# The last head prepares the next stage, values copied at mid-head, and a new order of turns, norms and transposes

## The reference

```
q, k, v = xn @ W_qkv                          # split in 16 heads
attn    = softmax(q k^T / 4 + spatial_bias)   # bias on tokens 1..256 alone
s       = (attn v) @ W_proj + b + layernorm(xn)
```

```
q, k, v = shift(x) @ wqkv
q, k    = rotary(l2norm(q) * qs), rotary(l2norm(k) * ks)
x       = x + softmax(mask(8 q k^T)) v @ wo
x       = x + (a * gelu(g)) @ w2 + b2,   a, g = layernorm(shift(x)) @ w1 + b1
```

## Time and profile before

| | us |
|---|---|
| median of 3 runs (lowest, highest) | 3201.47 (3199.73, 3202.40) |
| the profiled execution's own time | 3198.47 |
| its span, first to last instruction | 3196.5 |
| PE busy | 3056.0 (96%) |
| DVE busy | 2384.1 (75%) |
| ACT busy | 2236.8 (70%) |
| POOL busy | 846.4 (26%) |

### The profile page before, as it was taken

The page is one execution under the profiler, slowest core; times in us unless marked ns, Lnnn a source line. Parts: engine busy times, 40 slices in busy tenths (PEclk is TensorE's granted clock), DMA queues, the critical chain, the costliest instruction groups (busy, mean ns, idle before and its releaser), DMA issues.

```text
span 3196.5 us, 94351 instructions
## 1 busy us (share of the span) xinstructions
PE 3056.0 (96%) x37280; PEld 1985.2 (62%) x37280; DVE 2384.1 (75%) x4554; ACT 2236.8 (70%) x4645; POOL 846.4 (26%) x945
## 2 busy tenths in 40 slices
PE   8899999999999999999789999999999999999998
PEld 5444454444444444444367777777777777777776
DVE  8799989999899999899656666656665666656664
ACT  4588888888888888888556655665566556655564
POOL 5300000000000000000144434444344444444443
PEclk9899999999999999999889999999999999999999
DMA  7531111111111111111201100011100111011110
GB/s 236 174 105 49 36 44 45 45 43 40 45 45 45 40 40 48 45 45 35 83 11 42 39 26 29 28 41 39 31 26 30 38 39 34 25 33 33 41 38 4
DMA packets 157768, 153.48 MB, mean 48 GB/s; under 512 B 18144, under 2 KB 131128, under 8 KB 157496
## 3 DMA queue, kind: packets, MB, share of 16 engines
q1 hardware_dynamic: 157496, 149.52, 14.8%
HBM read 90.73 MB, written 58.72 MB: 47 GB/s over the span
## 4 chain that ended last, share of the span: by engine, by line
PE 85%; ACT 5%; issue 3%; DVE 3%; POOL 2%; SPq 1%; DMA 0%; POOLq 0%; DVEq 0%; ACTq 0%
PE banks L1347 15%; PE banks L1386 14%; PE banks L1403 14%; PE banks L1571 8%; PE banks L1453 7%; PE banks L1583 6%; PE banks L1499 4%; PE banks L1532 4%; PE banks L1542 4%; PE banks L1464 3%; PE banks L1511 3%; ACT kT L879 1%; ACT qT L872 1%; ACT vw L866 1%; PE banks L1521 1%
## 5 line engine op out<-in xcount | busy, mean ns | idle before, releaser
L1056 DVE TENSOR_REDUCE pair_max<-banks 128x1 f32<-128x1024 f32 x1039 | 1259.8, 1222 | 132.6 <-PE banks L1347 79.0
L837 ACT ACTIVATE probs<-banks 128x512 f32<-128x512 f32 x2057 | 1104.2, 599 | 171.5 <-PE banks L1386 164.8
L1347 PE MATMUL banks<-k_aug,q_aug 96*32 96x512 bf16 x8312 | 854.8, 385 | 6.1 <-ACT v_all L807 3.3
L1386 PE MATMUL banks<-q_aug,k_aug 98*32 98x512 bf16 x8228 | 846.8, 382 | 0.0
L1403 PE MATMUL banks<-probs,v_cur 128*32 128x256 f32 x8192 | 630.1, 380 | 31.1 <-POOL probs L614 31.1
L1347 PEld LDWEIGHTS banks<-k_aug,q_aug 96*32 96x32 bf16 x8312 | 239.7, 96 | 370.8 <-DVE pair_max L1056 215.5
L1386 PEld LDWEIGHTS banks<-q_aug,k_aug 98*32 98x32 bf16 x8228 | 251.8, 96 | 191.4 <-issue 3.5
L1571 PE MATMUL banks<-hnT,w_sb 128*114 128x128 f32 x3072 | 363.7, 275 | 0.9 <-ACT hnT L910 0.9
L1403 PEld LDWEIGHTS banks<-probs,v_cur 128*32 128x32 f32 x8192 | 260.7, 111 | 160.1 <-issue 37.9
L1571 PEld LDWEIGHTS banks<-hnT,w_sb 128*114 128x114 f32 x3072 | 344.9, 179 | 22.0 <-ACT hnT L910 22.0
L660 POOL TENSOR_TENSOR norms<-norms,half_power 128x8 f32<-128x8 f32 x128 | 210.3, 1643 | 442.0 <-DVE norms L1154 442.0
(11 more groups left out here) (141 smaller groups left out, 4022.9 us busy)
## 6 DMA issues: line engine op xcount, KB each, us to landing
acc_scratch<-acc_sb SPq DMA_DIRECT2D x128, 256.0 KB, 2.4
heads_win<-acc_scratch SPq DMA_DIRECT2D x512, 64.0 KB
q_aug<-q_parts SPq DMA_DIRECT2D x204, 64.0 KB, 2.2
k_aug<-k_parts SPq DMA_DIRECT2D x204, 64.0 KB, 2.2
q_parts<-parts SPq DMA_DIRECT2D x16, 384.0 KB, 3.0
k_parts<-parts SPq DMA_DIRECT2D x16, 384.0 KB, 3.9
x_in<-in_x SPq DMA_DIRECT2D x10, 512.0 KB, 4.5
xT_scratch<-xnT SPq DMA_DIRECT2D x8, 512.0 KB, 4.8
```

The source lines that it names most:

```text
L837: nc.scalar.activation(probs[:, step % PRING, :], banks[:, (use - first_use) % SRING, :], ACT.Exp, scale=SCALE).then_inc(prob_ready, 1)
L1056: nc.vector.tensor_reduce(pair_max[:, q, half:half + 1], banks[:, 4 + 2 * (t % 2):6 + 2 * (t % 2), :], AX.XY, ALU.max).then_inc(smax_read, 1)
L1347: last = nc.tensor.matmul(banks[m:m + CT, 4 + t % 4, :], q_aug[0:TERM_ROWS, b, q * P + m:q * P + m + CT], k_aug[0:TERM_ROWS, b, kq * BANK: ...
L1386: last = nc.tensor.matmul(banks[m:m + CT, (use - use_of(first_step)) % SRING, :], k_aug[0:AUG, b, kb * P + m:kb * P + m + CT], q_aug[0:AUG ...
```

## The change

It has four parts.

1. **Values.** POOL copies batch 0's values of the next head in the middle of a head, when batch 0's last value product is done; the bias products of batch 0 stand at the head of the loop and wait only for the exponentials.
2. **Last head.** The last turn ends at step 6 behind its head (its last copy of sums), with no scores, maximum tiles or shift rows of a further head.
3. **Seam.** The first windows and the rotary tables are loaded in the last head, behind its fourth group. POOL sets the constants of stage 3 and the tables in the last head. Behind `phase2_end` it zeroes only the first half of `kT` and `vw`, each with a semaphore of its own; `wo_sb` has one too. PE no longer waits for `phase2_end`.
4. **Stage 3.** PE transposes k, then q, then h(k), and projects v behind them. k's transposes go to bank 1, and `scores(0)` takes banks 0 and 1. ACT copies k, q, v in that order and squares q behind `cross`. DVE turns q before it sums its squares, and adds the attention between them. POOL, and no longer DVE, multiplies k by its inverse norms (`scale_k`), and inverts q's eight norms in two halves around the variance.

```diff
-    first = LH // 2 if n == 0 else 0
+    first = 0 if n == 0 else LH // 2
...
-    yield 0, range(FIRST_STEP)
-    for h in range(HEADS):
-        yield h, range(FIRST_STEP, FIRST_STEP + STEPS)
+    yield 0, range(FIRST_STEP), False
+    for h in range(HEADS - 1):
+        yield h, range(FIRST_STEP, FIRST_STEP + STEPS), False
+    yield HEADS - 1, range(FIRST_STEP, STEPS + SUMS_STEP + 1), True
...
+    for group in range(GROUPS):
+        store_sums(HEADS - 1, group)
+        if group == QC - 1:
+            for b in range(B):
+                load_window(0, b)
+            sp.dma_start(tables[:], rotary[0]).then_inc(tables_in, 16)
...
-    sp.dma_start(wo_sb[:], wo.rearrange("l (k p) e -> p l k e", p=P)).then_inc(ff_weights, 16)
+    sp.dma_start(wo_sb[:], wo.rearrange("l (k p) e -> p l k e", p=P)).then_inc(wo_in, 16)
...
     for b in range(B):
-        load_window(0, b)
         load_heads(0, b)
-    sp.dma_start(tables[:], rotary[0]).then_inc(tables_in, 16)
...
+    copy_values(0, 0)
+    pool.wait_ge(bias_ready, 1)
     with nc.gpsimd.Fori(0, HEADS) as h:
+        next_head = nc.gpsimd.snap((h + 1) % HEADS)
+        apply_bias(h, 0)
         pool.wait_ge(pv_done, h * PVH + 1)
-        for b in range(B):
...
+        copy_values(h, 1)
+        apply_bias(h, 1)
+        pool.wait_ge(pv_done, h * PVH + (PVH // 2 + 1))
+        copy_values(next_head, 0)
...
-    nc.gpsimd.sem_inc(phase2_end, 1)
-    pool.wait_ge(phase2_end, 4)
-    nc.gpsimd.memset(kT[:], 0.0).then_inc(ff_const, 1)
-    nc.gpsimd.memset(vw[:], 0.0).then_inc(ff_const, 1)
...
-    pool.wait_ge(ff_const, 10)
+    pool.wait_ge(ff_const, 8)
...
+    pool.wait_ge(ff_weights, FF_WEIGHTS)
+    pool.wait_ge(tables_in, 16)
+    for l in range(LAYERS):
+        rotary_table(l)
     for carried in (k_carried, v_carried, x_carried, x1_carried):
         nc.gpsimd.sem_inc(carried, ITEMS)
     nc.gpsimd.sem_inc(mask_set, 1)
-    pool.wait_ge(ff_weights, FF_WEIGHTS)
+    nc.gpsimd.sem_inc(phase2_end, 1)
+    pool.wait_ge(phase2_end, 4)
+    nc.gpsimd.memset(kT[:, :, :, :, 0:WINDOW], 0.0).then_inc(k_zeroed, 1)
+    nc.gpsimd.memset(vw[:, :, :, 0], 0.0).then_inc(v_zeroed, 1)
...
+    def invert_k(i, k):
+        invert_norms(i, k, 2, LH, 2 * LH)
+    def invert_q(i, k, n):
+        invert_norms(i, k, 4, n * (LH // 2), (n + 1) * (LH // 2))
+    def scale_k(i, k):
+        b = k % B
+        pool.wait_ge(inv_norms, at(i, k, 1, 3))
+        pool.wait_ge(k_added, at(i, k))
+        t8 = turned[:, b, 1].rearrange("p (h d) -> p h d", d=LD)
+        nc.gpsimd.tensor_tensor(t8, t8, norms[:, b, LH:].unsqueeze(2).to_broadcast([P, LH, LD]),
+                                ALU.mult).then_inc(k_turned, 1)
...
-    for l in range(LAYERS):
-        rotary_table(l)
-    invert_norms(0, 0, 1)
-    invert_norms(0, 0, 0)
+    invert_k(0, 0)
+    scale_k(0, 0)
+    for n in range(2):
+        invert_q(0, 0, n)
...
     for i, k, more in items(nc.gpsimd):
         widen_sums(i, k)
         if more:
-            invert_norms(i, k + 1, 1)
-            invert_norms(i, k + 1, 0)
+            invert_k(i, k + 1)
+            scale_k(i, k + 1)
+            invert_q(i, k + 1, 0)
         invert_deviation(i, k)
+        if more:
+            invert_q(i, k + 1, 1)
...
-            act.wait_ge(st_ready, h * ST_USES + (use + 2))
+            if ends and step >= STEPS:
+                if step == STEPS + SUMS_STEP:
+                    save_sums(h, group - 1)
+                continue
+            act.wait_ge(st_ready, h * ST_USES + (use + 2 - (ends and step > STEPS - KB + MSTEP)))
...
+            if kb == MSTEP and not (ends and group + 1 == GROUPS):
...
+        if n == 0:
+            act.wait_ge(q_crossed, at(i, k))
...
+                       banks[:, lanes(b) + 1, :].rearrange("p (j t) -> p j t", t=WINDOW)).then_inc(kT_kept, 1)
...
+            keep_k(i, k + 1)
+            keep_q(i, k + 1)
             keep_v(i, k + 1)
-            keep_q(i, k + 1)
-            keep_k(i, k + 1)
...
+            if ends and tile >= STEPS:
+                continue
...
+        if n == 1:
+            dve.wait_ge(squares_done, at(i, k, 1, 2))
+        else:
+            dve.wait_ge(qk_ready, at(i, k, 2, 2))
...
-        dve.wait_ge(k_added, at(i, k))
-        dve.wait_ge(inv_norms, at(i, k, 1, 2))
-        t8 = turned[:, b, 1].rearrange("p (h d) -> p h d", d=LD)
-        nc.vector.tensor_tensor(t8, t8, norms[:, b, LH:].unsqueeze(2).to_broadcast([P, LH, LD]),
-                                ALU.mult).then_inc(k_turned, 1)
...
+        dve.wait_ge(inv_norms, at(i, k, n + 2, 3))
...
             turn_k(i, k + 1)
             cross(i, k + 1, 0, q_crossed)
+            turn_q(i, k + 1)
+        add_attention(i, k)
+        if more:
             sum_squares(i, k + 1, 0)
-            turn_q(i, k + 1)
             bound_norms(i, k + 1, 0)
-        add_attention(i, k)
...
-            if step > first_step:
+            if step > first_step and not (ends and step >= STEPS):
...
-            if tile == STEPS:
+            if tile == STEPS and not ends:
                 pe.wait_ge(aug_loaded[0], h * AUG_LOADS + 2 * AUG_LOADS)
-            max_tile(h * PAIRS, tile)
+            if not (ends and tile >= STEPS):
+                max_tile(h * PAIRS, tile)
...
     pe.wait_ge(pv_done, HEADS * PVH + 1)
-    pe.wait_ge(prob_ready, HEADS * STEPS + (FIRST_STEP + 1))
     nc.tensor.sem_inc(phase2_end, 1)
-    pe.wait_ge(phase2_end, 4)
-    pe.wait_ge(ff_const, 12)
+    pe.wait_ge(prob_ready, HEADS * STEPS + 1)
+    pe.wait_ge(acc_saved, HEADS * GROUPS + 1)
+    pe.wait_ge(smax_read, HEADS * PAIRS + 2)
+    pe.wait_ge(ff_const, 10)
     pe.wait_ge(ff_weights, FF_WEIGHTS)
...
+            last = nc.tensor.transpose(banks[:, lanes(b) + 1, j * P:(j + 1) * P],
...
+        if k == 0 and n == 0:
+            pe.wait_ge(k_zeroed, 1)
         if n == 0:
-            pe.wait_ge(v_kept, at(i, k))
             pe.wait_ge(kT_kept, at(i, k))
             pe.wait_ge(qT_kept, at(i, k))
+            pe.wait_ge(squares_done, at(i, k, 2, 2))
+        else:
+            pe.wait_ge(v_kept, at(i, k))
...
+        if k == 0:
+            pe.wait_ge(v_zeroed, 1)
...
+        if k == 0:
+            pe.wait_ge(wo_in, 16)
...
         if more:
-            project_v(i, k + 1)
+            transpose_k(i, k + 1)
             transpose_q(i, k + 1)
         transpose_h(i, k)
         if more:
-            transpose_k(i, k + 1)
+            project_v(i, k + 1)
             scores(i, k + 1, 0)
         transpose_normed(i, k)
         if more:
```

More of the change, by code:

```diff
@@ L257, in build @@
         ff_const = sem("ff_const")
+        k_zeroed = sem("k_zeroed")
+        v_zeroed = sem("v_zeroed")
+        wo_in = sem("wo_in")
         tab_ready = sem("tab_ready")
@@ L649, in move, with invert_norms @@
                 return nc.gpsimd.tensor_tensor(dst, src, ones.to_broadcast(shape), ALU.mult)
-            def rotary_table(l):
-                nc.gpsimd.tensor_tensor(tab[:, l], tables[:], gains[:, l], ALU.mult).then_inc(tab_ready, 1)
-            def invert_norms(i, k, n):
+            def invert_norms(i, k, sums, first, last):
                 b = k % B
-                norm = norms[:, b, n * LH:(n + 1) * LH]
-                pool.wait_ge(norm_sums, at(i, k, 4 - 2 * n, 4))
-                nc.gpsimd.tensor_tensor(norm, norm, half_power[:], ALU.pow).then_inc(inv_norms, 1)
+                norm = norms[:, b, first:last]
+                pool.wait_ge(norm_sums, at(i, k, sums, 4))
+                nc.gpsimd.tensor_tensor(norm, norm, half_power[:, 0:last - first], ALU.pow).then_inc(inv_norms, 1)
+            def invert_k(i, k):
[9 more added lines that the diff above has]
+                                        ALU.mult).then_inc(k_turned, 1)
             def carry_keys(i, k):
@@ L829, in _ @@
             nc.scalar.activation(bias_exp[:], dist[:], ACT.Exp, scale=dmax[:, 4:5]).then_inc(dist_exp, 1)
-            for h, steps in turns():
+            for h, steps, ends in turns():
                 first_use = use_of(steps[0])
@@ L1087, in _ @@
             nc.vector.memset(bias_exp[0:1, 0, :], 1.0).then_inc(bias_ready, 1)
-            for h, steps in turns():
+            for h, steps, ends in turns():
                 for step in steps:
-                    group, kb = step // KB, step % KB
                     tile = step + LEAD
+                    if ends and tile >= STEPS:
+                        continue
                     if tile % 2 == 1:
@@ L1264, in _ @@
             cross(0, 0, 0, q_crossed)
+            turn_q(0, 0)
             sum_squares(0, 0, 0)
-            turn_q(0, 0)
             bound_norms(0, 0, 0)
@@ L1434, in _ @@
                         scores_to_exp(h, first_step, step)
-                    if kb == MSTEP:
+                    if kb == MSTEP and not (ends and group + 1 >= GROUPS):
                         shift_rows(h, first_step, group + 1, use_of(step) + 1)
             pe.wait_ge(pv_done, HEADS * PVH + 1)
```

(9 more changed lines are left out.)

70 lines of the change are left out of this document (35 added, 35 removed).

## The result

The changed kernel takes 3108.3 us (median of four runs, 3107.5 to 3109.8), the kernel before 3201.9 in the same series. The ratio is 0.9709, with a 95% interval from 0.9692 to 0.9726: 2.9% faster. Forecast were 3089 and a range from 3076 to 3130. The profiled execution took 3108.16 us with a span of 3106.4; the span of before was 3196.5, so 90.1 us went from the span where the forecast had 112.3.

A forecast was written before the change was run, and what follows sets the result against it. PE was taken as the bound of stages 2 and 3, its idle time and the seam as the gain. 31.0 + 4.4 + 32.2 + 44.7 = 112.3 off 3198.47 gives 3086.2, with the 3.0 offset 3089 us; range 3076 to 3130.

The forecast's parts named there:

- Values at mid-head: Start of heads 1 to 15 in stage 2: PE's wait for POOL's bias products goes, 2.07 us each, 31.0 us.
- the clock: Stage 2: without the stall, three of fifteen heads no longer run long at PE's half clock, 3 x 1.45 = 4.4 us.
- head 0's wait: Stage 2, head 0: about 6 us of the 31.1 us wait, not touched by the change; gain 0 to 6, taken as 0.
- Last head and seam: End of stage 2 to stage 3's first scores: these start at 1572.2 instead of 1604.44, 32.2 us won.
- Stage 3: Each item's PE wait ahead of the next scores for ACT's copy of k goes: 0.71 us in 63 items, 44.7 us.
- rooms: Stage 3, spare time before PE would wait: k 0.8, q 0.1, h 0.15, normalised rows 0.2 us; so no new wait.
- q at 2091.41, room 0.1: Stage 3: PE reaches q's transposes at 2091.41, q's sum is done at 2091.3, so PE doesn't wait.
- The gelu chain "0.2 more room": Stage 3: scores 0.9 us earlier give the gelu chain 0.2 more room; worth 0 to 4 us, taken as 0.
- rival 1: Stage 3: POOL's power of four columns costs what eight cost; 23 us back, 3112; chance 0.13.
- rivals 2 and 5: Stage 3: 2, `scale_k` takes 2.54, 35 us back, 3124, chance 0.07; 5, POOL bounds the first half, 3247 at 4.5, chance 0.02.
- rival 3: Stage 2: a stall of the same length stays at the head's start; 31 + 4 us less gain, 3124; chance 0.07.
- The offset of 3.0: Whole kernel: the median of the runs lies 3.0 us above the profiled execution, which turns 3086.2 into 3089.

## Why the prediction was right, and where it was too large

- **Values at mid-head (31.0) and the clock (4.4): together 29.7.** The mechanism was right: the stall is gone, head 0's wait stays, and the three long heads with their half clock are gone too. The clock's term holds: these heads were 90.6 long and the twelve ordinary ones 89.1. Mis-sized is the 2.07 us a head. An ordinary head went from 89.1 to 87.46, 1.66 less. The 2.07 was measured as the stalled group's length less an ordinary one's and left the group at 10.87, "nothing else is late at that place"; in fact 11.23 remain. PE's restart of the ring and its order at a turn's first step had stood in the shadow of POOL. The timeline of the kernel before shows the second of these waits, inside the eight records that the prediction counted at full pace from 583.92:

```profile
584.35 0.10 PEld L1347 LDWEIGHTS banks<-k_aug,q_aug 96*32 96x32 bf16 x4 [0.52 <-DVE pair_max L1056]
```

  So the second maximum tile only starts there, and POOL's part of the stall is 0.2 us shorter than 2.05. The runs show that with both waits taken away a head has 87.09 us, the forecast 87.0.
- **Last head and seam (32.2): 30.5.** From the last bias products to PE's first projection 42.2 were forecast (1519.52 to 1561.7) and 42.9 measured; from there to the scores 10.5 and 11.56. The second difference is v's projection, 3.5 us at the half clock, where I had taken a value in the lower half of 1.73 to 3.46. The order held, and so did the costs: `scale_k` 1.03 (1.15 forecast), k's norms 1.69 (1.64).
- **Stage 3 (44.7): 30.8.** The wait for ACT's copy of k went, as forecast. Two of the rooms were not there. *q at 2091.41, room 0.1*: q's sum was ready when forecast, 4.10 us behind the start of its projection (2091.3 - 2087.20 forecast, 2021.56 - 2017.46 measured). Wrong was PE's time. The forecast took 2090.97 from the chain, the modelled end of `project_o`. In the timeline of the kernel before PE starts its next step 0.16 earlier:

```profile
2090.81 1.88 PE L1464 MATMUL banks<-wqkv_sb,xT 128*128 128x512 f32 x4
```

  So PE is ready for q's transposes at 2021.51, ahead of the sum (2021.56), and they start 0.14 behind it, for which the forecast had nothing either. A room of 0.1 was smaller than each of these errors.

  The same reading left out 0.17 us of gain: by starts the old way to the scores is 3.70 and the new one would be 2.81 (0.44, 0.44, 0.22 and 1.72), 0.89 less. Of that k's step keeps 0.15, in which PE waits for q, q's own step 0.05, and v's projection up to the scores 0.09 (1.81); why the last is longer isn't shown. What is left is 0.59, where the forecast had 0.71: 7.7 us.

  *The gelu chain "0.2 more room"*: the room is 0.15 less. This was the wrong sign of a term taken as 0, and costs 63 x 0.145 = 9.1 us. PE comes to the projection 0.03 sooner behind the scores, and the chain there got longer by 0.11: DVE starts 1.49 behind them on the mean, 1.38 before (1.52 and 1.40 in the items shown: 2025.74 - 2024.22 and 2095.91 - 2094.51). The scores themselves take as long as before. Between the semaphore that they raise and DVE's first instruction lie 0.33 us on the mean, before 0.23, and in that time DVE's queue has two or three instructions of its own, before one or two. The one more belongs to its wait for the inverse norms, which the change altered from two steps an item to three:

```profile
L1208 DVEq ALU_OP  x1: 45/45/45, 2025.4 to 2025.4; - x1
```

  In the kernel before that wait (L1162) adds no instruction there, and in the run with the old last stage the time is 0.23 again. No run changed this wait alone, so it is the trace's account and no test.

  7.7 and 9.1 less the 3.2 won elsewhere (0.03 an item, 1.3 in item 0) are 13.6 of the 13.9 missing.
- **Rivals.** The power of four columns is 1.02, as by the line (rival 1 falls), and `scale_k` 1.04 (rivals 2 and 5 fall). No stall of 2 us stays at the head's start, only 0.4 (rival 3 in small).

  The rule of the Trainium skill, page "SBUF — State Buffer", section "Who interferes with whom", spoke of a DVE instruction with two SBUF operands beside a GpSimd one. The prediction said that no row shows such a pair. Stage 1, which isn't changed, has them in both traces; this is the timeline of the changed kernel:

```profile
60.79 2.28 POOL L606 TENSOR_TENSOR parts<-rest,parts 128x512 bf16<-128x512 f32 x2
...
62.09 1.00 DVE L1026 SCALAR_TENSOR_TENSOR between<-between,total 128x4 f32<-128x4 f32 x1
```

  The kernel before has the same DVE instruction at 62.60 with no POOL work beside it, and there it takes 0.16. Here it ends at 63.09, 0.02 behind POOL's. Sixteen short DVE instructions of stage 1 are held in this way in the changed kernel (0.52 to 1.16 us, each ending 0.02 or 0.03 behind POOL's instruction), so the trace agrees with the rule. The seam has a pair that does not follow it: DVE's L1186 runs at 1538.39, POOL's power L685 until 1538.86. They take 0.69 and 1.69 us, against 0.68 and 1.64 in stage 3, so neither waited for the other's end. The kernel before has one such pair too (1597.52), with the same two times. Why a power doesn't hold DVE isn't shown, and POOL's spans are rough. In stage 3 no such pair meets (`scale_k` ends at 2020.33, q's sum starts at 2020.87), so the rule cost nothing there, as forecast. Beside a slower `scale_k`, a multiplication, q's sum could have been held.
- **The offset of 3.0** between profile and median was right for before and is 0.1 after. Without it the forecast would have been 3086.
- **The range.** 3108 lies in it, but its upper end had been set by rivals 1 to 3, and none of these came true. That the terms which were too large fit in the room left for others is in part luck.

## What to carry over

A long wait hides the shorter ones that end inside it. Before the whole of it is counted as gain, list every semaphore and every re-used bank that the waiting engine passes in the same step, with the time at which each is free. Two waits that share one place can each look harmless, or even useful, when the other is removed alone: try both edits together before either is dropped. Take the time at which an engine is ready from the starts of its instructions, not from the end of the one before. And a stage in which one engine is 98% busy still has gains in its hand-overs: handing on two blocks instead of four was worth 19 us, in a chain that the forecast had taken as 0.

## What was not expected of the hardware

- PE's granted clock fell to 0.58 in the window from 1541 to 1545, after 3.1 us without a matmul (ahead of k's transposes at 1540.33), while the stalls of 2 us of the kernel before led to the half clock in three heads of fifteen only.
- A power on POOL costs 1.64, 1.02 and 0.55 us for 8, 4 and 1 columns on 128 partitions: 0.4 and 0.155 a column.
- A short DVE instruction with two SBUF operands took 1.00 instead of 0.16 us beside a subtraction of POOL and ended with it, and the same kind of instruction ran in its usual 0.69 beside a power of POOL.
- The wait that one moved instruction causes can be larger than the gap it leaves: PE's scores, a few instructions earlier in its queue, turned a weight load's wait of 0.43 us into 1.33.
